# Routed experts at the end of a transformer block: layer-norm roots refined in two tile steps instead of four, two row tiles normalised a step, output scatters paced nine tiles behind a group of four instead of twelve

## What is computed

```python
x = x + layernorm(attention(layernorm(x)))      # 16 heads of 8, relative keys and values
t = layernorm(x).reshape(8192, 128)
logits = t @ w_router.T                         # 16 experts, the best one per token
shared = silu(t @ w_gate.T) * (t @ w_up.T) @ w_down.T
scaled = sigmoid(best logit) * t
gate, up = split(scaled @ gate_up_proj[e])      # e: the expert of the token; 128 x 512
expert = (up * silu(gate)) @ down_proj[e]       # 256 x 128
x = x + layernorm(shared + expert)              # no scale, no bias; per token
```

## Time and profile before

| | |
|---|---|
| median of 3 runs | 1610.67 us (1607.13 to 1612.69) |
| the profiled execution's own time | 1612.52 us |
| its span, first to last instruction | 1610.8 us |
| PE busy | 1509.4 us, 94% |
| DVE busy | 1228.3 us, 76%, 3580 instructions |
| ACT busy | 1115.4 us, 69% |
| POOL busy | 482.2 us, 30% |
| mean granted TensorE clock | 0.983 of full speed |

### The profile page before, as it was taken

The page is one execution under the profiler, slowest core; times in us unless marked ns, Lnnn a source line. Parts: engine busy times, 40 slices in busy tenths (PEclk is TensorE's granted clock), DMA queues, the critical chain, the costliest instruction groups (busy, mean ns, idle before and its releaser), DMA issues.

```text
span 1610.8 us, 67870 instructions
## 1 busy us (share of the span) xinstructions
PE 1509.4 (94%) x28642; PEld 1178.3 (73%) x28642; DVE 1228.3 (76%) x3580; ACT 1115.4 (69%) x2053; POOL 482.2 (30%) x678
## 2 busy tenths in 40 slices
PE   5789999998999999999999999999999999899993
PEld 2347777776778777877787777777878766568993
DVE  7996768787878887888788878887887335644997
ACT  4537767776777777777777777777776766236882
POOL 4532130223122312231223122312201101664576
PEclk9999999999999999999999999999999999999997
DMA  3468576765464456444544464445424562425561
GB/s 86 145 192 224 137 179 161 192 152 157 106 151 103 114 125 156 102 112 125 154 104 110 125 154 102 119 119 146 101 56 104 123 211 73 122 86 155 152 176 56
DMA packets 489136, 212.11 MB, mean 132 GB/s; under 512 B 330663, under 2 KB 462436, under 8 KB 488832
## 3 DMA queue, kind: packets, MB, share of 16 engines
q1 hardware_dynamic: 474112, 165.75, 42.2%
q0 software_dynamic: 14720, 42.03, 7.8%
HBM read 105.73 MB, written 102.85 MB: 129 GB/s over the span
## 4 chain that ended last, share of the span: by engine, by line
PE 64%; DVE 21%; SPq 5%; issue 4%; DMA 3%; ACT 2%; POOL 1%; ACTq 0%; DVEq 0%; POOLq 0%
PE pv L891 12%; DVE mx L1405 11%; PE mix L846 10%; PE sc L869 7%; PE rel L898 7%; PE sc L871 6%; PE mix L848 5%; PE sc L863 4%; PE sc L1054 2%; SPq L584 2%; PE rel L1000 1%; PE mix L908 1%; PE pv L1061 1%; PE mix L774 1%; PE sc L990 1%
## 5 line engine op out<-in xcount | busy, mean ns | idle before, releaser
L1146 ACT ACTIVATE w<-sc,escale 128x512 f32<-128x512 f32 x1024 | 685.9, 689 | 300.3 <-PE sc L871 176.2
L1405 DVE TENSOR_REDUCE mx<-mix 128x1 f32<-128x512 f32 x960 | 642.6, 683 | 187.3 <-PE mix L848 176.2
L846 PE MATMUL mix<-WE 128*32 128x512 f16 (+1 forms) x1968 | 388.8, 394 | 27.8 <-DVE mx L1405 16.4
L891 PE MATMUL pv<-w,shared_part 128*9 128x128 f32 x8192 | 373.1, 274 | 4.4 <-issue 4.4
L869 PEld LDWEIGHTS sc<-shared_part,Wt 96*128 96x128 f16 x5120 | 219.9, 97 | 81.5 <-issue 31.8
L848 PE MATMUL mix<-Wn,WE 128*32 128x350 f16 (+41 forms) x1968 | 275.7, 281 | 0.3 <-issue 0.3
L869 PE MATMUL sc<-shared_part,Wt 96*128 96x64 f16 x5120 | 258.1, 192 | 4.2 <-DVE mx L1405 1.9
L891 PEld LDWEIGHTS pv<-w,shared_part 128*9 128x9 f32 x8192 | 202.8, 90 | 75.2 <-issue 49.2
L898 PE MATMUL rel<-w,shared_part 128*32 128x128 f32 x5120 | 257.2, 273 | 0.0
L871 PE MATMUL sc<-shared_part 104*128 104x128 f16 x2560 | 247.6, 218 | 0.3 <-issue 0.3
L1131 ACT ACTIVATE WE<-qp,hmask 128x256 f16<-128x256 f16 x500 | 215.6, 499 | 21.2 <-PE sc L848 21.2
(11 more groups left out here) (266 smaller groups left out, 1967.0 us busy)
## 6 DMA issues: line engine op xcount, KB each, us to landing
qm_d<-ks POOLq DMA_DIRECT2D x48, 512.0 KB, 5.0
shared_part<-qm_d SPq DMA_DIRECT2D x32, 768.0 KB
kt_d<-ks SPq DMA_DIRECT2D x48, 256.0 KB
shared_part<-kt_d SPq DMA_DIRECT2D x128, 96.0 KB
xs_d<-zrow SPq DMA_DIRECT2D x5, 2056.0 KB, 11.5
vs_d<-vst SPq DMA_DIRECT2D x16, 576.0 KB
shared_part<-vs_d SPq DMA_DIRECT2D x32, 288.0 KB
orl_d<-rel_s SPq DMA_DIRECT2D x512, 8.0 KB
```

Source lines behind the costliest of these rows:

```text
L846: nc.tensor.matmul(nat[rows, :], lq[:, rows], kn[b2][:, at:at + S], start=True, stop=False, skip_group_check=True)
L891: mm = nc.tensor.matmul(pv[b2][32 * g:32 * g + 9, P * hh:P * hh + P], VC[j][:, b2, 0 if near else 1, h, :], wt[:, :, b2, h, :], start=(j = ...
L1146: nc.scalar.activation(weights, products, ACT.Exp, scale=escale[:, 0:1]).then_inc(s["exp_done"], 1)
L1405: nc.vector.tensor_reduce(mx[:, k:k + 1], nat[:], AX.X, ALU.max).then_inc(s["mx_done"], 1)
```

## The change

The refinement puts two steps of the chain in each third, six in a tile step, and so ends after two tile steps (REFINE_TILES). Normalising takes two tiles a step for an ending of four and four for one of eight, over two steps, and raises `fin_step` twice an ending instead of four times; the waits on it are counted anew. The two residuals follow in the step after each half. The wait ahead of a group's first shared add now asks for all normalising of group g - 2. The loop runs four steps less. STORE_AT is 9: tile m of a four-tile ending is scattered when m + 13 down projections are done.

```diff
--- before.py
+++ after.py
@@ -1707,7 +1707,8 @@
                 return
             if k == 0:
                 dve.wait_ge(ysh_ld[g % 2], 16 * (g // 2 + 1))
-                at_least(dve, m["fin_step"], 4 * (g - 2) + 1)
+                if g >= 2:
+                    dve.wait_ge(m["fin_step"], 2 * FINISHED[g - 2])
             nc.vector.tensor_tensor(yg[g % 2][:, k, :], y_p[n % 3], ysh[g % 2][:, k, :], ALU.add).then_inc(m["y_ev"], 1)
 
         def add_first_shared():
@@ -1772,19 +1773,19 @@
             dve.wait_ge(m["oidx_step"], 2 * g + 2)
             nc.vector.tensor_copy(oidx[g % OUT_RING][:], oidx_f[g % OUT_RING][:]).then_inc(m["oidx_rdy"], 1)
 
-        def expert_normalize(f, quarter):
+        def expert_normalize(f, half):
             g, k0, size = ENDINGS[f]
-            if quarter == 0:
+            if half == 0:
                 dve.wait_ge(m["root3"], REFINE_STEPS * (f + 1))
                 if k0 == 0:
                     at_least(dve, out_st[g % OUT_RING], 16 * GROUP * (g // OUT_RING))
-            for k in range(k0 + size // 4 * quarter, k0 + size // 4 * (quarter + 1)):
+            for k in range(k0 + size // 2 * half, k0 + size // 2 * (half + 1)):
                 ins = nc.vector.tensor_scalar(og[g % OUT_RING][:, k, :], yg[g % 2][:, k, :], mv3[g % 2][:, k, 0:1], rstd3[g % 2][:, k:k + 1], ALU.subtract, ALU.mult)
             ins.then_inc(m["fin_step"], 1)
 
         def residual(f, half):
             g, k0, size = ENDINGS[f]
-            dve.wait_ge(m["fin_step"], 4 * f + 2 * half + 2)
+            dve.wait_ge(m["fin_step"], 2 * f + half + 1)
             tiles = slice(k0 + size // 2 * half, k0 + size // 2 * (half + 1))
             nc.vector.tensor_tensor(og[g % OUT_RING][:, tiles, :], og[g % OUT_RING][:, tiles, :], x1g[g % 2][:, tiles, 0:D], ALU.add).then_inc(m["out_rdy"], 1)
 
@@ -1792,20 +1793,19 @@
 
             g, k0, size = ENDINGS[f]
             since = step - (GROUP * g + k0 + size + (5 if g else 6))
-            if 0 <= since < REFINE_STEPS // 3:
-                refine(f, 3 * since + third)
-            since -= REFINE_STEPS // 3
+            if 0 <= since < REFINE_TILES:
+                for k in range(2):
+                    refine(f, 6 * since + 2 * third + k)
+            since -= REFINE_TILES
             if third == 2:
                 if since == -1 and k0 == 0:
                     places(g)
-                if since == 2:
-                    residual(f, 0)
-                if since == 4:
-                    residual(f, 1)
-                if 0 <= since < 4:
+                if 1 <= since < 3:
+                    residual(f, since - 1)
+                if 0 <= since < 2:
                     expert_normalize(f, since)
 
-        for n in range(SORTED + 5 + REFINE_STEPS // 3 + 5):
+        for n in range(SORTED + 5 + REFINE_TILES + 3):
             for third in range(3):
                 for f in range(len(ENDINGS)):
                     ending(f, n, third)
@@ -2067,8 +2067,9 @@
 AHEAD = 4
 TICKS = 4
 SCATTER_TICK = 7
-STORE_AT = 12
+STORE_AT = 9
 REFINE_STEPS = 3 + 9
+REFINE_TILES = REFINE_STEPS // 6
 WHOLE = 2
 ENDINGS = [(g, 0, GROUP) for g in range(WHOLE)] + [(g, k0, GROUP // 2) for g in range(WHOLE, GROUPS) for k0 in (0, GROUP // 2)]
 FINISHED = [sum(g <= last for g, _, _ in ENDINGS) for last in range(GROUPS)]
```

## The result

The changed kernel is slower. Its six runs have a median of 1624.05 us (1618.82 to 1629.07) beside 1612.24 for the kernel before; the ratio is 1.0076, 95% interval 1.0048 to 1.0105. The direction and the mechanism were forecast, the size was not: 1624.05 lies just past the end of the stated range, 1624. Two later measurements of the same kernel, beside other runs of the kernel before, gave 1.0055 [1.0032, 1.0079] and 1.0062 [1.0043, 1.0081], that is 1620.3 and 1620.8 us where before had 1611.0; these two lie inside the range.

A forecast was written before the change was run, and what follows sets the result against it. DVE's own issue was taken to bound the routed experts from tile 21, POOL's scatter issue the tail. Terms 10.7 + 0.35 - 3.9 = +7.2 us put the median at 1618, range 1611 to 1624.

The forecast's parts named there:

- The bound: Routed experts: DVE's own issue sets the pace from tile 21, POOL's issue of 16 scatters sets the tail.
- Part 1: Refinement in pairs on DVE: the second step waits for the first, 0.12 us more a pair, 89 pairs, +10.7 us.
- rival A: Refinement on DVE: pairing is free, so 0.35 - 3.9 = -3.5 us, 1607, faster than before; chance 0.12.
- The row of 0.29: One refinement pair in the tail, 0.29 us between starts; set aside for 0.19, used only in the upper bound of 19.6.
- Part 2: DVE work that comes earlier, between the products of tiles 21 and 79: +0.35 us; before tile 21 nothing.
- Part 3: Uneven tile steps in the routed experts cause no idle: 0; +3.5 us if one buffer less counts.
- Part 4: Scatters at 9, not 12, in the tail: 13 left after the last down group, not 16, -3.9 us.
- The sum: All terms of the routed experts together: 10.7 + 0.35 - 3.9 = +7.2 us.

The follow-up runs named there:

- e3: Changed kernel with one refinement step a third instead of two, the rest of the change kept: stage 89.48 us, tail 19.59, ratio 1.0013 to the kernel before.
- e6: Changed kernel with one refinement step a third, each split into two instructions for half its tiles: ratio 1.0049 to the kernel before, on a chip with stalls.
- e15: Kernel before with only STORE_AT changed from 12 to 9: stage 87.62 us, tail 21.51, ratio 1.0007.
- e2: Changed kernel with STORE_AT back from 9 to 12: stage 101.16 us, tail 22.23, ratio 1.0079 to the kernel before.
- e4: Kernel before with only the refinement in pairs over two tile steps, pace 12: stage 102.30 us, tail 22.30, ratio 1.0124.
- e18: Changed kernel with four refinement steps a tile step, each between others' work, over three tile steps: stage 91.04 us, tail 18.48, ratio 1.0005 to the kernel before.

## Why the prediction was right or wrong

**The bound** was read rightly. DVE's distances between starts set the stage: undoing the pairs (e3) gives 10.9 us back, and without dependence even twice the instructions start at 0.07 (e6). The mechanism was right; the step that failed is the size of one term.

**Part 1, the pairs: the term that was mis-sized.** The neighbours' distances came as forecast (0.18 to 0.20), so rival A is dead. But 10.7 us should have been 12.3, 0.138 for a pair and not 0.12. Two things were missing: the start behind the second step is 0.08 away and not 0.07 (0.9 us in all), and a completion that is waited for is exposed to the scatters (0.7 us). The row of 0.29, which I set aside as a lengthened record, was of this second kind of cost: it ends at 1594.83, 1.04 after the start of a scatter (1593.79).

The rule of the Trainium skill that I weighed there ("VectorE: DVE Perf Modes", The DRAIN you can't avoid, by which a semaphore behind each of eight copies costs nothing more) isn't borne out for a dependent neighbour among small tiles: with an unchanged count of instructions the stage grew by 12.66 us. The advice to minimise the count of instructions stands on the same page of the Trainium skill in Rules for kernel authors, not in the section that the prediction names.

**Part 2**, work that comes earlier, +0.35: 0.28 of it are the four more refinement steps, which stand within the +12.63; the residuals came to 0.06 more, as forecast. Before tile 21 nothing was lost: tile 14 to tile 21 took 11.16 us, where it took 11.11.

**Part 3**, no idle of DVE from uneven steps: right, its only idles are the short ones inside the pairs and in `places`. In e3, though, where DVE is lighter, uneven steps did cost something, at most 1.7 us.

**Part 4: right sum, wrong reason.** 13 scatters and 17.6 us (forecast 17.4) came out. But I gave the 3.9 us to the pace alone. They need two things at once: pace 9 without the earlier rows gives 0.3 (e15), the earlier rows without pace 9 give nothing (22.23 in e2), both give 3.5. The step failed in that it counted scatters by their gate on the down projections and only checked that the rows would be ready after the change; the same check on the kernel before would have shown that with pace 9 the rows are the later of the two there (with pace 12 the down projections are, by 0.5 us: ending 14's first residual is done at 1587.22 and the last down group at 1587.71).

**The sum** within the stage and tail was +7.2 and is +9.1. The six runs say +12 and the later ones +9.3 and +9.8. The forecast was 1618 and the six runs gave 6.05 more: 1.9 from the sum, 1.6 because before's own median moved from 1610.67 to 1612.24, and the remaining 2.6 is within their scatter. The range ended at 1624.0 because it took in the scatter of three runs (5.6 us) where the kernel's executions lie over some 10. That the first six runs fall 0.05 us outside it and the two later measurements inside is chance; the term of 10.7 was too small in all of them.

## What to carry to other kernels

On an engine that is bound by its starts, price an instruction by the distance to the next start, and that by who the next one is: unrelated 0.07 us, dependent 0.19, for the same 0.15 us record. A chain of small steps belongs between other work. Moving it together to finish sooner cost more than it gave wherever the engine had other work (the changed kernel, e4); no run here shows a case in which it pays. And where two conditions hold back the same work, find out which one is later before crediting a change to either.

## What was not expected of the hardware

Some small DVE instructions last until the record of one of POOL's indirect scatters (0.98) ends. In the kernel before, all eight refinement records over 0.22 us between 1500 and 1584 end 0.98 to 1.04 us after a scatter's start. The longest began 0.52 after the scatter at 1529.14:

```profile
1529.66 0.46 DVE L1753 TENSOR_SCALAR rstd<-var 128x4 int32<-128x4 int32 x1
```
```profile
1529.14 0.98 POOL L2007 DMA_INDIRECT out_dram<-w,oidx  x1 [0.30 <-issue]
```

It depends on the instruction as well as on the moment. Of the refinement steps that start 0.60 to 0.75 after a scatter, all TENSOR_SCALAR ones are lengthened (five of five before, six of six in the changed kernel) and none of the others (of eight and six); in e4 six of the others are, all L1759. A smaller lengthening stands at the scatter's start: in e3 and e18 15 of the 19 steps that start 0.03 us or less before it last 0.20 to 0.23. With plain stores, whose POOL record takes 0.54, there are three records over 0.22 in both kernels together, and they end 0.5 us after a store's start. It costs little until something waits for the end: before's stage is 87.76 with the scatters and 87.42 without.

The Trainium skill ("SBUF — State Buffer", SBUF: two separate sides) describes a port pair that DVE and GpSimd lock for a whole instruction, the loser fully blocked: on DVE's side an instruction in a two-port mode, or, against a GpSimd instruction that reads SBUF, one with two SBUF inputs. The trace agrees that they meet, but a refinement step that starts within the first 0.5 us of a scatter's record lasts 0.22 us at most, and a hold is some 0.3 us at most; whether it is that lock isn't shown.

The stalls of up to 6 us on two chips were in all the kernels that ran there and weren't explained.
